# One line in the quantised attention of a two-layer perceiver: the second batch's mix begins three woven places later

## The reference, cut to what matters

```python
x = x + _L0_xattn_ref(_layernorm(x), ctx_2048, Wq, Wk, Wv, Wo)        # 16 heads of 128
x = x + _L0_attn_ref(_layernorm(x), W_in, b_in, W_out, b_out, ...)    # the "mix": it normalises again inside
x = x + _L0_ffn_ref(_layernorm(x), gate_w, expert_w, expert_b)        # 8 experts, the best 2
x = x + _L1_xattn_ref(_layernorm(x), ctx_2048, Wq, bq, Wkv, ...)      # 16 heads of 16, quantised, 4096 keys
x = x + _L1_attn_ref(_layernorm(x))                                   # dilated attention in segments of 64
x = x + _L1_ffn_ref(_layernorm(x), w_gate, w_up, w_down)              # block-quantised feed-forward
```

## Time and profile before

| what | value |
|---|---|
| median of 3 runs | 736.98 us (735.31 to 737.95) |
| the profiled execution | 736.12 us |
| its span | 734.8 us, 13080 instructions |
| DVE, PE, ACT, POOL busy | 572.5, 657.4, 372.1, 298.5 us |
| mean granted TensorE clock | 0.967 |
| reductions of the firsts (line 1550) | 256 of 679 ns |
| exponentials (line 1621) | 128 of 1202 ns |

### The profile page before, as it was taken

One profiled execution on the slowest core, in us unless ns is written; L12 is line 12 of the kernel. 1 busy time (PEld: TensorE's weight loads), 2 busy tenths in 40 slices (PEclk: granted clock), 3 DMA queues, 4 the chain that ended last, 5 costly groups with the idle time before them and its releaser, 6 DMA issues. The chain is left out here.

```text
span 734.8 us, 13080 instructions
## 1 busy us (share of the span) xinstructions
PE 657.4 (89%) x4834; PEld 416.9 (57%) x4834; DVE 572.5 (78%) x1045; ACT 372.1 (51%) x584; POOL 298.5 (41%) x399
## 2 busy tenths in 40 slices
PE   4899999999999979999999998968998998788843
PEld 3456676666666756766776665744553444334421
DVE  3698976977786777688898656577989999999655
ACT  4544334333433434344443424418868998787811
POOL 3185534463455431666663134425324332223100
PEclk9999999999999999999999999998999999999965
DMA  9366787756655657998767738737989999789900
GB/s 296 109 140 134 161 172 161 166 127 139 127 140 129 148 145 208 181 208 185 148 162 148 172 82 178 146 117 159 179 128 165 176 197 188 143 141 162 181 0 8
DMA packets 347152, 111.22 MB, mean 151 GB/s; under 512 B 313544, under 2 KB 344528, under 8 KB 346832
## 3 DMA queue, kind: packets, MB, share of 16 engines
q1 hardware_dynamic: 347088, 110.39, 72.0%
HBM read 32.23 MB, written 0.26 MB: 44 GB/s over the span
## 5 line engine op out<-in xcount | busy, mean ns | idle before, releaser
L871 PE MATMUL psum<-c_nat,eT 128*128 128x256 f16 x1536 | 189.2, 274 | 0.7 <-ACT u_sb L1002 0.7
L845 PE MATMUL psum<-cT,qk 128*128 128x512 f16 x768 | 171.0, 379 | 1.2 <-ACT cT L765 1.1
L1621 ACT ACTIVATE cT<-psum,bias,q_scale 128x1024 f16<-128x1024 f32 x128 | 153.4, 1202 | 35.8 <-PE psum L1534 22.4
L871 PEld LDWEIGHTS psum<-c_nat,eT 128*128 128x128 f16 x1536 | 150.8, 98 | 27.0 <-issue 1.2
L1550 DVE TENSOR_REDUCE tops<-psum 128x1 f32<-128x512 f32 x256 | 158.4, 679 | 9.4 <-PE psum L1534 9.2
L1534 PE MATMUL psum<-kT,v_space 128*128 128x512 f16 x512 | 142.0, 386 | 18.8 <-DVE tops L1550 12.5
L845 PEld LDWEIGHTS psum<-cT,qk 128*128 128x128 f16 x768 | 74.9, 98 | 86.1 <-ACT cT L765 1.3
L1039 DVE TENSOR_REDUCE neg_max<-psum 128x1 f32<-128x2048 f32 x32 | 73.2, 2288 | 34.5 <-PE psum L845 34.3
L1534 PEld LDWEIGHTS psum<-kT,v_space 128*128 128x128 f16 x512 | 45.3, 98 | 86.6 <-DVE tops L1550 53.8
L1027 DVE TENSOR_TENSOR e_lo<-e_all,e_hi 128x2048 f16<-128x2048 f32 x32 | 84.2, 2631 | 0.0
L708 ACT ACTIVATE qT<-psum 128x128 f32<-128x128 f32 x32 | 8.9, 278 | 130.6 <-PE psum L690 130.4
(11 more groups left out here) (232 smaller groups left out, 849.4 us busy)
## 6 DMA issues: line engine op xcount, KB each, us to landing
wq_h<-in_L_xattn_Wq SPq DMA_DIRECT2D x32, 128.0 KB, 2.4
wk_h<-in_wkT SPq DMA_DIRECT2D x32, 128.0 KB, 2.4
wv_h<-in_L_xattn_Wv SPq DMA_DIRECT2D x32, 128.0 KB, 2.4
wo_h<-in_L_xattn_Wo SPq DMA_DIRECT2D x32, 128.0 KB, 2.5
mx_land<-in_mx_weights SPq DMA_DIRECT2D x8, 384.0 KB, 3.8
v_space<-in_ctx SPq DMA_DIRECT2D x4, 512.0 KB, 7.8
cT<-in_ctx SPq DMA_DIRECT2D x2, 1024.0 KB, 10.5
c_nat<-in_expert_wT SPq DMA_DIRECT2D x2, 1024.0 KB, 7.1
```

Of the source, the lines that this page charges most:

```text
L845: ins = pe.matmul(s_ps[:, n * 512:(n + 1) * 512], c.qk[:, u % 2, q_part, k, :], m.cT[:, b, c_part, 4 * n:4 * n + 4, k, :], start=(k, q_par ...
L871: ins = pe.matmul(u_ps, c.eT[:, v % 2, e_part, j, :], m.c_nat[:, v // H0, c_part, j, :], start=(j, e_part, c_part) == (0, 0, 0), stop=(j, ...
L1621: act.activation(x.y[:, u % 2, q * CHUNK:(q + 1) * CHUNK], m.bank(3 + 2 * (q % 2), 2), ACT.Exp, bias=m.bias[:, u:u + 1], scale=m.q_scale[: ...
```

## The change

The three steps ahead of the weave (norm, again, scaled) move from slots -5, -4, -3 to 0, 1, 2, and the woven steps of the mix are counted from 4 (`NC`) and not from 1.

```diff
@@ -2039,7 +2039,7 @@
             x, y, z, w = MixTiles(nc, local, 1), AttentionTiles(nc, local, m), DilatedTiles(nc, local), \
                 FeedTiles(nc, local, m)
             room = Room(m.bank(7)[:, D:2 * D], shared=True)
-            mix = dict(norm=-5, again=-4, scaled=-3) | woven(MIX_WOVEN, 1)
+            mix = dict(norm=0, again=1, scaled=2) | woven(MIX_WOVEN, NC)
             experts = dict(norm=mix["out"]) | woven(EX_WOVEN, mix["out"] + 1)
             queries = dict(norm=experts["bias"]) | woven(QU_WOVEN, experts["bias"] + 1)
             output = woven(OUT_WOVEN[0], queries["qT"] + 1) | woven(OUT_WOVEN[1], NC * (H1 + 1) + 1)
```

## The result

The changed kernel takes 730.22 us (median of 6 runs, 728.24 to 730.89) against 736.06 us (6 runs, 734.55 to 737.95) beside it. The ratio is 0.9918 with a 95% interval of 0.9893 to 0.9943, a gain of 736.06 x 0.0082 = 6.0 us, with 4.2 to 7.9 from the ends of the interval. The forecast was a gain of 5.1. The start of the weave moves by three places, but slot 4 is skipped, so every woven step moves by four, one whole unit.

The account below looks back on a forecast made before the run. After a start held by the bias queued behind the normalisation, DVE's reductions set the pace. n 31 moves from 511.24 to 506.05, a gain of 5.2 us; against the median, 736.98 - 5.1 = 731.9 us, range 729.5 to 734.6.

Parts of the forecast that it names:

- Step 1: GpSimd, start of quantised attention: bias 0 has nothing before it, ACT starts 7.3 us earlier, a ceiling and not the gain.
- Step 2: DVE: norm, again, scaled go ahead of n 13, 15, 17; reductions hide both roots, n 17 starts near 495.2.
- Step 3: GpSimd: gamma and beta end at 496.8, bias 1 goes ahead of them, bias 2 near 501.6 is covered by 0.9 us.
- Step 4: PE: xT at 498.0 without the 5.3 us stall; DVE stalls near 0.4 us at qkv0 and 0.8 at qkv2.
- n 31 at 506.05: DVE: reduction n 31, behind the qkv2 add, starts at 506.05 us where it was 511.24 before; gain 5.2 us.
- Step 5: SyncE: first transposing DMA issued near 491.6 behind loads landing near 496.9, wanted by the attend at 502.9; costs nothing.
- The other way round: Second sum: steps from qkv2 on 0.4 us earlier, then one free unit of 4.78 us fewer before slot 69; again 5.2.
- The clock rival: PE at the stage's start: clock falls though the long stall is gone, costing 1 to 2.4 us, 732.9 to 734.3; chance 0.25.
- The rival by which ACT keeps its whole head start: Start of the stage: ACT's lateness may have slowed DVE; gain up to 7.3 us, 729.7; chance 0.07.
- The rival that gives the gain back: GpSimd's `least` steps slip behind gamma and beta, DVE waits at each qkv step; loses 3 us and more, 735 to 737; chance 0.08.
- The slower rival: First transposed halves land too late behind loads, holding the attend; landing after 508.1 cancels the gain, worst 743 us; chance 0.05.

Follow-up runs that it names:

- ACT's start alone: Against the kernel before, norm, again and scaled stand right behind bias 0 on GpSimd, weave still from slot 1; 734.68 us, ratio 0.9977.
- DVE in one piece: Against the kernel before, bias first on GpSimd and weave from slot 4, but norm, again, scaled uninterrupted on DVE before n 13; 732.50 us, ratio 0.9937.
- second profile: The changed kernel run and profiled once more, nothing altered; 731.12 us, ratio 0.9912 to the kernel before.
- doubled loads: Against the changed kernel, the 2,048 KB of expert weights loaded a second time, ahead of the first transposing DMA; 735.60 us, ratio 1.0001 to the kernel before.
- loads split: Against the changed kernel, expert weights loaded in four parts behind the transposing DMAs of units 1 to 4, other loads behind unit 5's; 734.28 us, ratio 0.9921.
- products spread: Against the changed kernel, three empty places among the eight expert products, so a unit holds two and not three; 732.36 us, ratio 0.9920.
- qT's leave later: Against the changed kernel, PE waits for ACT's four query copies one slot later, first output half one slot later; 729.69 us, ratio 0.9884.

## Why the prediction was right, point by point

The forecast of 731.9 (a gain of 5.1) met 730.22 (a gain of 5.8 by medians, 6.0 by the ratio), inside the range of 729.5 to 734.6.

- *Step 1, the bias costs nothing and ACT's 7.3 us are a ceiling.* Right: ACT gained 7.15 us and the kernel 6, and with ACT's start alone the gain was 2.07.
- *Step 2, DVE's reductions hide the roots.* Right in order and sign. n 17 was put 6.4 us after the add and came at 5.9, as reductions begin before the end of what stands ahead of them. What the cover is worth is at most the 2.6 us between the kernel with DVE in one piece and the changed one, since the clock fell at the start of the former only.
- *Step 3, GpSimd's queue.* Bias 1 was to be out about 6.0 after the add and was out at 6.0, bias 2 about 12.8 and was out at 12.2. ACT waited for neither.
- *Step 4, PE and qkv.* xT was put at 9.2 after the add and came at 8.7, without a wait. The stall at qkv0 was put at 0.4 and was 0.17, the one at qkv2 at 0.8 and was 0.66. The term "n 31 at 506.05" was mis-sized by 0.8 us: on that scale it came at 505.24. Therefore 6.0 at this point and not 5.2, and -1.23 instead of the forecast 0.4 us in the steps that follow.
- *Step 5, the DMA costs nothing.* Right in the end, but by luck. The step took 496.9, the landing of the expert weights, for the end of the loads. Three more loads follow them; in the changed kernel the last one landed 10.05 us after the add (498.8 on the prediction's scale) and the first half 1.9 us behind it. It had 1.2 us in hand instead of several, and the second half, which the step doesn't look at, 0.04.
- *The other way round, one free unit fewer.* Shown by the constant -1.23 over nine units and then 4.78 more: 5.99 us at bias 16 in the second profile, 5.00 in the first, where the clock fell. At bias 31 it is 5.48 in the second, where the clock fell between biases 26 and 27 (1.0 us), and 5.78 in the first.
- *The clock rival* (1 to 2.4 us): at the start it stayed full in both profiles of the changed kernel, so the 2.4 us that the prediction worked out for the rule of the Trainium skill, TensorE: Matmul & The Clock Gate, "A second HAM failure mode: psum-queue depth-cycling", did not come about there. That is partly luck. The prediction took nothing because no microsecond would be nearly empty, and one was: PE was busy 14% from 491 to 492. In three other kernels with the same head the clock did fall there; in two of them the price can be read, 0.66 and 0.84 us by bias 3. Against three profiles of six the chance of 0.25 looks low, and the upper end of 2.4 was too high. An estimate for the changed kernel with such a fall is a gain of 6.0 - 0.8 = 5.2, which is the forecast's sum only because step 4 was 0.8 us too slow. (The range's upper end, 734.6, is called that of this rival, but its sum gives 736.98 - 2.7 = 734.3.)
- *The rival by which ACT keeps its whole head start*: no, 6.0 of 7.15 us.
- *The rival that gives the gain back*: no, the stalls at the qkv steps were smaller than my own.
- *The slower rival*: its mechanism exists and was forced. A first half that landed 16.7 us after the add (505.5 on the prediction's scale) cancelled the gain, together with the falls of the clock beside it. The prediction asked for a landing after 508.1, and PE begins to wait from a landing 1.2 us later than the changed kernel's.

## What to carry to other kernels

Look in each in-order queue for a short instruction that many wait for and that stands behind a long chain it doesn't need, and then ask what the freed engines will wait for next. Here three moves had to be made at once. Of the two that could be tried alone, one was worth 2 us and the other nothing. A shift of woven work by whole units of the loop keeps all its local timing, and then only the number of free units and the start have to be counted. Compare variants by a landmark within the stage, counted from its beginning, where totals scatter by more than the effect, and look for clock falls and late DMAs in each profile before crediting a difference to the change.

## What the runs showed of the hardware

- A transposing DMA issued while 2,532 KB of loads were in flight took 8.9 us to land where 4.3 to 5.2 was usual without them, and 13.3 us with another 2,048 KB in front. In both kernels it landed 1.9 us behind the last load. The Trainium skill, DMA: Bandwidth & Descriptors, "Queues, rings and completion order", says that descriptors are taken in ring order on each engine; the 4.4 us more for 2,048 KB more agree.
- SyncE was held as well: issuing that DMA took it 6.85 us, and 11.18 us with the doubled loads, against 1.97 us with the loads split and out of the way. The next transposing DMA waited behind it in the queue.
- The granted clock fell behind the same 1.3 us wait in some executions and not in others (1.89 against 1.04 us for four matmuls), and 1.0 us of the unit's time went with it. One profile can't tell whether a change has removed or added such a fall.
- At the start of the stage the clock stayed full in both profiles of the changed kernel and in the kernel with the products spread; in the three others that issue the same woven head (qT's leave later, loads doubled, changed with the loads split) it fell about 6 us after the add and stayed at its lower level for some 3 us.
